# Wide attention in rounds of two supersteps, with keys, maxima and values in three shared PSUM banks

## What is computed

```python
xn = _layernorm(x, ln_gamma, ln_beta)
q = (xn @ w_q).reshape(B, SQ, NUM_HEADS, DIM_HEAD)
kv = context @ w_kv
k, v = jnp.split(kv, 2, axis=-1)
...
scores = jnp.einsum('bhqd,bhkd->bhqk', q * SCALE, k)
attn = jax.nn.softmax(scores, axis=-1)
out = jnp.einsum('bhqk,bhkd->bqhd', attn, v).reshape(B, SQ, INNER)
```

## Time and profile before

| | us |
|---|---|
| median of 3 runs | 4161.85 (4158.45 to 4163.68) |
| profiled execution, its own time | 4167.73 |
| span of its instructions | 4165.9 |

### The profile page before, as it was taken

How to read it: one execution, slowest core, us unless ns; L and a number is a source line. 1 busy time by engine, 2 the same in 40 slices (tenths; PEclk the granted TensorE clock), 3 DMA queues, 4 the chain that set the end, 5 groups by cost and what they waited for, 6 DMA issues and landing times. The chain is left out here.

```text
span 4165.9 us, 80943 instructions
## 1 busy us (share of the span) xinstructions
PE 3670.1 (88%) x30262; PEld 2604.2 (63%) x30262; DVE 2490.6 (60%) x3308; ACT 2304.7 (55%) x4294; POOL 1660.6 (40%) x1365
## 2 busy tenths in 40 slices
PE   5899999999999999999776995799999987667399
PEld 3677777777777777777544894455555543333298
DVE  5566556565665565555165212478787777467587
ACT  3566666666666666666333211266666666435165
POOL 2576667666666666666412102210111000024033
PEclk9999999999999999999887997799999999879599
DMA  6777777767776776665111483878788754100011
GB/s 218 271 254 248 250 255 258 258 243 262 256 253 245 258 251 226 227 234 189 55 35 60 164 311 138 237 165 178 168 178 166 149 79 65 21 11 1 20 45 43
DMA packets 231715, 723.26 MB, mean 174 GB/s; under 512 B 47373, under 2 KB 128525, under 8 KB 162445
## 3 DMA queue, kind: packets, MB, share of 16 engines
q1 hardware_dynamic: 228640, 709.70, 54.7%
q0 software_dynamic: 2688, 8.39, 0.6%
HBM read 623.61 MB, written 94.37 MB: 172 GB/s over the span
## 5 line engine op out<-in xcount | busy, mean ns | idle before, releaser
L760 POOL TENSOR_TENSOR wa_acc<-wa_acc,wa_probs 128x512 f32<-128x512 f32 x960 | 1254.3, 1307 | 485.3 <-ACT wa_probs L616 374.0
L680 DVE TENSOR_REDUCE wa_mx<-wa_ps_m 128x2 f32<-128x1024 f32 x512 | 627.1, 1225 | 458.8 <-PE wa_ps_m L488 456.0
L616 ACT ACTIVATE wa_probs<-wa_ps_s 128x512 f32<-128x512 f32 x1024 | 529.8, 602 | 538.1 <-PE wa_ps_s L530 534.1
L1299 DVE TENSOR_REDUCE na_mx<-na_ps_m 128x2 f32<-128x1024 f32 x512 | 613.9, 1220 | 202.8 <-PE na_ps_m L1120 199.4
L1244 ACT ACTIVATE na_probs<-na_ps_s 128x512 f32<-128x512 f32 x1024 | 556.0, 595 | 315.8 <-PE na_ps_s L1140 313.4
L608 ACT ACTIVATE wa_ps_s<-wa_m_wide 128x512 f32<-128x512 f32 x1024 | 576.2, 602 | 1.0
L509 PE MATMUL wa_ps_o<-wa_probs,wa_values 128*64 128x256 f32 x4096 | 498.5, 385 | 1.0 <-ACT wa_probs L616 1.0
L452 PE MATMUL wa_ps_k<-wa_k_ctx,wa_w_k 128*128 128x512 f32 x1488 | 417.9, 416 | 0.0
L475 PE MATMUL wa_ps_m<-wa_w_v,wa_v_ctx 128*128 128x256 f32 x2880 | 380.2, 283 | 1.3 <-DVE wa_mx L680 1.3
L475 PEld LDWEIGHTS wa_ps_m<-wa_w_v,wa_v_ctx 128*128 128x128 f32 x2880 | 360.2, 190 | 28.4 <-DVE wa_mx L680 6.7
L509 PEld LDWEIGHTS wa_ps_o<-wa_probs,wa_values 128*64 128x64 f32 x4096 | 271.3, 136 | 154.5 <-issue 12.9
(11 more groups left out here) (344 smaller groups left out, 5711.9 us busy)
## 6 DMA issues: line engine op xcount, KB each, us to landing
wa_k_ctx<-ctx_split SPq DMA_DIRECT2D x248, 1024.0 KB, 4.9
wa_v_ctx<-ctx_split SPq DMA_DIRECT2D x120, 1024.0 KB, 6.8
na_ctx<-ctx_split SPq DMA_DIRECT2D x56, 1024.0 KB, 11.3
na_keys<-k_rows SPq DMA_DIRECT2D x384, 128.0 KB
ctx_split<-wa_stage SPq DMA_DIRECT2D x32, 1024.0 KB, 4.8
wa_land<-in_ctxT SPq DMA_DIRECT2D x32, 512.0 KB, 8.2
ge_w_b<-in_w_rows SPq DMA_DIRECT2D x8, 2048.0 KB
k_rows<-na_k_high SPq DMA_DIRECT2D x64, 256.0 KB, 3.0
```

Of the source, the lines that this page charges most:

```text
L616: act.activation(probs[:, c % R:c % R + 2, h * SQ:(h + 1) * SQ], ps_s[n % BANKS][:, :].rearrange("p (c n) -> p c n", c=2), ACT.Exp).then_i ...
L680: dve.tensor_reduce(mx[:, half, :, k], ps_m[:, :, :], AX.X, ALU.max).then_inc(m_taken, 1)
L760: pool.tensor_tensor(to[:, :], to[:, :], probs[:, c % R, :], ALU.add).then_inc(summed, 1)
L1299: dve.tensor_reduce(mx[:, half, :, k], ps_m[n % 2][:, :, :], AX.X, ALU.max).then_inc(m_taken, 1)
```

## The change

The loop is still over supersteps, but the work is laid out in rounds of two:

- At an even `j` TensorE does maximum half 0, scores, maximum half 1, then **two** key blocks and **all** the units of values of the round (none, two or three). At an odd `j` it does maximum half 0, scores, maximum half 1, and then weighs **both** supersteps, `j - 1` and `j`. The denominator goes ahead of these, in `st` = 1.
- `ps_m` and `ps_k` become three single banks `ps_x`. The heads of a maximum half lie in two of them, the key blocks in banks 1 and 2, units of values in 0, 1, 2 (1 and 2 where the maxima are turned, which takes bank 0). `maximum_banks` picks the banks.
- Each half is reduced by two instructions, one a head, with a count of `m_taken` for each, and every matmul waits for no more than the bank that it overwrites.
- ScalarE takes the two key blocks between the initial values; VectorE reduces both halves before anything else, does the reciprocal in `st` = 5 and the product in `st` = 7, and copies the numerator and the denominator apart. The maxima are turned one superstep earlier (`st` = 6). SP's issues are put in another order within the round.

The core of the diff:

```diff
-        ps_m = s.ps("ps_m", [P, 2, 512])
-        ps_k = s.ps("ps_k", [P, 512])
+        ps_x = [s.ps(f"ps_x{i}", [P, 512]) for i in range(3)]
...
-            n = CG + j + 2
-            return n if CG <= n < G * CG else None
+            return [] if j % 2 else [n for n in (CG + j + 2, CG + j + 3) if n < G * CG]
...
+        def maximum_banks(j, half):
+
+            last = 1 if j % 2 and len(value_units(j - 1)) == 2 and not turning(j - 1) else 2
+            return (0, 3 - last) if half == 0 else (last, 0)
...
                 if of_max is not None:
-                    maximum(*of_max, 1)
-                if kb is not None:
-                    project_keys(kb)
-                if st == SS - 1 and a + 1 < G:
-                    pe.wait_ge(m_taken, maxima_through(j))
+                    pe.wait_ge(m_taken, reduced[1])
+                    if value_units(j - 1):
+                        pe.wait_ge(v_ready, values_before(j))
+                    elif key_blocks(j - 1):
+                        pe.wait_ge(kl_ready, keys_before(j))
+                    maximum(*of_max, 1, maximum_banks(j, 1))
+                for i, kb in enumerate(kbs):
+                    pe.wait_ge(m_taken, reduced[2 + i])
+                    project_keys(kb, ps_x[1 + i])
+                if turning(j):
+                    pe.wait_ge(m_taken, reduced[4])
                     turn_maximum(a + 1)
...
-                if j >= 1:
+                if j % 2 and st == 1 and j > 1:
+                    denominator(a - 1)
+                if j % 2 and 0 < j < LAST:
                     weigh(j - 1)
-                if st == 0 and j > 0:
-                    denominator(a - 1)
+                    weigh(j)
...
-                dve.tensor_reduce(mx[:, half, :, k], ps_m[:, :, :], AX.X, ALU.max).then_inc(m_taken, 1)
+                for h in range(2):
+                    dve.tensor_reduce(mx[:, half, h, k:k + 1], ps_x[banks[h]][:, :], AX.X, ALU.max).then_inc(m_taken, 1)
...
-                dve.tensor_copy(o_raw[:, :], ps_o[:, :]).then_inc(o_copied, 1)
+                dve.tensor_copy(o_raw[:, 0:SQ], ps_o[:, 0:SQ]).then_inc(num_copied, 1)
```

More of the change, by code:

```diff
@@ L451, in project_keys @@
                     for part, of in ((0, 0), (0, 1), (1, 0)):
-                        ins = pe.matmul(ps_k[:, :], w_k[g % 2][:, part, c, :], source[:, of, c, :],
+                        ins = pe.matmul(bank[:, :], w_k[g % 2][:, part, c, :], source[:, of, c, :],
                                         start=(n == 0), stop=(n == 3 * KD - 1))
@@ L496, in turn_maximum @@
                         col = h * SQ + half * P
-                        ins = pe.matmul(ps_m[:, 1, col:col + P], m_neg[:, 2 * half + h, :], ident[:, :], start=True, stop=True)
+                        ins = pe.matmul(ps_x[0][:, col:col + P], m_neg[:, 2 * half + h, :], ident[:, :], start=True, stop=True)
                 ins.then_inc(mT_done, 1)
@@ L628, in _ @@
                 a, st = j // SS, j % SS
-                turning = st == SS - 1 and a + 1 < G
-                kb = key_block(j)
+                kbs = key_blocks(j)
                 if j >= 0:
@@ L633, in _ @@
                         exponents(4 * j + n)
-                if j >= -1 and not turning:
+                if j >= -1:
                     initial(4 * j + 4)
-                if kb is not None:
-                    take_keys(kb)
-                if turning:
+                if kbs:
+                    take_keys(kbs[0], ps_x[1])
+                if j >= -1:
+                    initial(4 * j + 5)
+                    initial(4 * j + 6)
+                if kbs:
+                    take_keys(kbs[1], ps_x[2])
+                if j >= -1:
+                    initial(4 * j + 7)
+                if turning(j):
                     take_maximum(a + 1)
-                    initial(4 * j + 4)
-                if j >= -1:
-                    for n in range(1, 4):
-                        initial(4 * j + 4 + n)
                 if j >= 0 and st == 1 and a < BLOCKS - CG:
@@ L721, in _ @@
                     split_low(k + 2)
-            take_maximum(0, CG - 1, 0)
-            take_maximum(0, CG - 1, 1)
-            for j in range(-2, LAST + 4):
+            take_maximum(0, CG - 1, 0, (0, 1))
+            take_maximum(0, CG - 1, 1, (0, 1))
+            for j in range(-2, LAST + SS):
                 a, st = j // SS, j % SS
-                of_max, kb = max_block(j), key_block(j)
+                of_max, kbs = max_block(j), key_blocks(j)
                 if of_max is not None:
-                    take_maximum(*of_max, 0)
-                if st == 1 and j > 1:
-                    copy_out(a - 1)
-                if of_max is not None:
-                    take_maximum(*of_max, 1)
+                    take_maximum(*of_max, 0, maximum_banks(j, 0))
+                    take_maximum(*of_max, 1, maximum_banks(j, 1))
+                if st == 0 and j > 0:
+                    copy_numerator(a - 1)
+                if st == 2 and j > 2:
+                    copy_denominator(a - 1)
+                if turning(j):
+                    finish_maximum(a + 1)
+                if kbs:
+                    take_keys(kbs[0], ps_x[1])
```

160 lines of the change are left out of this document (90 added, 70 removed).

## The result

| | median us (range, runs) | ratio to before, 95% interval |
|---|---|---|
| before | 4160.15 (4157.59 to 4163.68, 4) | |
| after | 4063.26 (4061.25 to 4072.41, 4) | 0.9771 [0.9754, 0.9788] |

The change takes 97 us off. The profiled execution took 4062.29 us (span 4060.4), against 4167.73 for the one of before, which lay 7.6 above its median; so the two traces differ by 105 us and the medians by 97.

What follows compares the result with a forecast made beforehand. TensorE was taken to bound the attention, busy 1592.86 of 1600 us, with gaps at phase boundaries. Terms of -101 + 2 + 1 + 1 = -97 us, taken from the median 4161.85, gave 4065 us, range 4050 to 4112.

Steps and rivals of the forecast that it cites:

- Gate of M1: Second maximum half needs only one head's reduction (0.69 us), so starts 1.43 us after the scores instead of 1.58.
- The round: Two supersteps with two value units in all, phases joined: 13.66 us instead of 14.52, saving 0.86 a round.
- The lead of 0.10: First weight load of a key block: 0.10 us extra, not paid by the second of two adjoining key blocks.
- The round without V: Rounds without value units: 11.5 us instead of 11.64, saving 0.14, with some new waits.
- What is added: Extra VectorE reductions at most 0.63 us a round, opening 0 to 2.5 us, late value copies 2 us in all.
- What is moved: Reordered engine and SP work stays covered; key loads land in 4.7 to 9.0 us and are needed 12 us later.
- The cover of the second W: Second weighing comes 0.41 us later than its exponentials need, so it does not wait.
- A: VectorE's order makes maximum halves late again: 4085 to 4125 us, middle 4098; chance 0.23.
- B: Second weighing waits for its exponentials, slower than before: 4183 us; chance 0.06.
- C: TensorE's granted clock at 1.2 GHz part of the time: gain gone at 5.5%, 4205 us at 8%; chance 0.03.
- D: No change: gates move elsewhere and give back what the phase boundaries save; chance 0.04.
- E: Values to next maximum and second maximum half to weighing cheaper than their neighbours: 4045 us; chance 0.06.

Runs made afterwards that it cites:

- one_wait: Kernel before, with the second maximum half no longer also waiting for the rounded keys: 4138.3 us.
- one_reduction: Changed kernel, but each maximum half is again emptied by one reduction over both banks, for which the next half waits: 4125.6 us.
- exp_twice: Changed kernel with one more exponential, into a spare tile, ahead of each odd superstep's exponentials: 4070.16 us.
- store_behind: Changed kernel, with the split context block's store issued behind the key loads in 21 of 24 rounds: 4054.21 us, and 4057.13 when repeated.
- maximum_between: Changed kernel, but in the odd superstep the second maximum half stands between the two weighings: 4122.1 us.

## Why the prediction was right, step by step

The time (4065 forecast, 4063.26 measured) and the place (the attention ends at 1935 forecast, 1934.0 measured) came as forecast. By its own terms:

1. **Gate of M1: right.** S to M1 is 1.43 in even and 1.44 in odd supersteps, M1 to K 0.32 to 0.34, and of 200 to 1700 us no wait of a matmul for M1 is listed. The new reduction takes 0.685 us (0.69 taken, 0.61 the other bound): in the groups from 200 to 1700 us, which answer to the earlier trace rows,

```profile
L714 DVE TENSOR_REDUCE wa_mx<-wa_ps_x 128x1 f32<-128x512 f32 x851 | 547.3, 685 | 307.5 <-PE wa_ps_x L500 307.5
L686 DVE TENSOR_TENSOR wa_stage<-wa_land,wa_stage 128x1024 fp32r<-128x1024 f32 x23 | 28.3, 1231 | 0.0
```

   What was incomplete is the reason. The 0.15 of lateness was read as one wait for one reduction; 0.09 of it came from which instruction carried the open wait (one_wait). With the gate gone neither shows, so the number held.

2. **The round: right, 13.64 for 13.66.** The two K take 888.75 to 891.61 = 2.86 instead of 1.51 + 1.41 = 2.92. The lead of 0.10 is there: single matmuls of the first K, and the first of the second K,

```profile
889.08 0.39 PE L465 MATMUL wa_ps_x<-wa_k_ctx,wa_w_k 128*128 128x512 f32 x1
...
890.24 0.62 PE L465 MATMUL wa_ps_x<-wa_k_ctx,wa_w_k 128*128 128x512 f32 x2
```

   start 0.33 and 1.49 behind the first (888.75). What was mis-sized is the time between K's other matmuls: the second K takes 1.37 (0.228 a matmul), not 1.41, and the first 1.49, not 1.51. That is some 7 us of gain in 120 rounds that the sum lacked. A third of it goes with the late M1: with the gate back (one_reduction) the two K take 2.88. V to M0' is 2.96, the two W 3.61 for 3.60, M1' to W 0.33: at the lower of its bounds.

3. **The round without V: right in size.** K to M0' is 3.12 (3.15 forecast):

```profile
990.41 3.02 PE L465 MATMUL wa_ps_x<-wa_k_ctx,wa_w_k 128*128 128x512 f32 x12
...
993.53 0.51 PE L500 MATMUL wa_ps_x<-wa_keys_high,wa_qh 64*128 64x512 f32 x2
```

   The rest was less exact: S' to M1' is 1.77 instead of 1.43, the 0.3 for the initial value, but the 0.2 for VectorE didn't come. The prediction's own terms add up to 11.43, not 11.5, and measured the round takes 11.74 with a D in it, about 11.3 without. Sixteen supersteps take 112.74 for 112.7. TensorE no longer waits for the maxima: the 14 waits of 0.5 us at M0 are gone.

4. **What is added: too high by about 3.** The low split of a context block takes 1.23 us instead of 1.67, and V to M0' is 2.96 in rounds with and without it, so the 2 us for the 24 split rounds aren't there. The last +1 of the sum has no term of its own. The opening costs nothing that can be seen: the 17th maximum starts at 192.48 after and at 192.88 before.

5. **What is moved: cover right, SP wrong.** The cover of the second W is 0.46 for 0.41 (exp_twice), and M1' was not held up. The step that failed is "A stored context block goes ahead of them in 24 rounds, with 9 us left: enough". I took the slowest landing of before, 9.0, as the worst case of the new order too. There one key load was issued at a time; here the second load has a store and a load ahead of it, landed after 10.6, and about 7.1 us went in 13 rounds (store_behind gets 7 to 8 back). The closer K of step 2, of the same size and the other sign, hid this in the sum: without late loads sixteen supersteps take 112.2, as the last three groups show, which have none, and with them the average is the 112.7 that was forecast. That this agrees to 0.1 us is luck.

The rivals. A (VectorE takes part back) did not come; one_reduction shows its price, 62 us with both halves gated. B did not come by itself and came when its cover was removed. C, the clock, stayed at 1.00 from 200 to 1900 us; by the Trainium skill's rule ("TensorE: Matmul & The Clock Gate", "A second HAM failure mode: psum-queue depth-cycling"), weighed in the prediction, three shared banks were a candidate for a swinging clock, and the trace of after doesn't bear it out either. D (no change) is ruled out by the interval. Of E, M1' to W came at its cheap bound and V to M0' no cheaper than taken; the time is far from 4045.

One caution on the agreement: the forecast of −97 was a sum over the attention, and there the traces show −100, so the sum was 3 us short. That the medians differ by 97 owes the last 3 us to the variation of the unchanged rest.

## What to carry to other kernels

On an engine that is full, read starts, not busy time: each phase boundary has a price (a change of shape, a weight load that a late matmul exposes, an open wait that stands ahead of the weight load instead of on it), and fewer, longer phases save it, as long as what each phase waits for is given enough work in front. When work is grouped so, ask of every consumer what stood between it and its producer and stands there no longer; W' behind M1' cost 156 us. When loads are grouped, price the last one of the group with all that its queue holds ahead of it, not by the landing of a load that went alone.

## What the hardware showed that I had not expected

- Which instruction carries the wait that opens last is worth 0.09 us. With that wait in an instruction of its own and a satisfied one on the weight load behind it, the matmul starts 0.14 after the reduction's end; with the open wait on the weight load, 0.05, also where a satisfied one stands ahead of it (one_wait, one_reduction). Over the 248 supersteps with a second maximum half behind scores that was 20 us.
- The parts of a change need not add. The rounds bring 13 us with the gate in place and 51 beside free banks; the banks bring 45 alone and 62 within the rounds, because each part covers waits that the other has alone.
- The same low split on VectorE (128x1024) took 1.67 us on average before and 1.23 after. The average hides two lengths: before, 12 of 23 took 2.09 and 11 took 1.22; after, 22 of 23 took 1.22. They go by the GpSimd addition that is running when the split starts: in all of them, before and after, the split ends 1.08 to 1.11 us after that addition's end.

```profile
454.26 1.28 POOL L760 TENSOR_TENSOR wa_acc<-wa_acc,wa_probs 128x512 f32<-128x512 f32 x1
454.54 2.09 DVE L653 TENSOR_TENSOR wa_stage<-wa_land,wa_stage 128x1024 fp32r<-128x1024 f32 x1
```

  Here (a trace of before) the addition ends at 455.54 and the split at 456.63. The short ones start 0.1 us before an addition's end. The long negated maxima of maximum_between fit the same reading: 943.44 + 1.29 = 944.73, and they end at 945.03. No run moves the two against each other on purpose, so this is read from the traces and not tested.
